# Single picks, ScalarE's copies and paired scores in the narrow attention of a two-layer decoder kernel

## The reference

```python
def _L1_attn_ref(x, g_q, Wq, bq, g_kv, Wkv, bkv, g_head, Wo, bo):
    HEAD = 16; HD = 16
    q = (_rms(x, g_q) @ Wq + bq).reshape(B, T, H, d).transpose(0, 2, 1, 3)
    kv = (_rms(x, g_kv) @ Wkv + bkv).reshape(B, T, 2, H, d)
    ...
    scores = jnp.einsum('bhqd,bhkd->bhqk', _rms(q, g_head), _rms(k, g_head)) * scale
    attn = jax.nn.softmax(scores, axis=-1)
    wv = jnp.einsum('bhqk,bhkd->bhqd', attn, v)
    out = wv.transpose(0, 2, 1, 3).reshape(B, T, D) @ Wo + bo
# the mixture's sum over the picks, which lands in x just ahead of it:
routed = jnp.einsum('enh,ne->nh', y, comb)
x = x + (routed + sg * shared)
x = x + _L1_attn_ref(_layernorm(x, axis=-1), ...)
x = x + _L1_xattn_ref(_layernorm(x, axis=-1), ctx_2048, ...)
```

## Time and profile before

| | us |
|---|---|
| median of 3 runs | 1902.86 |
| lowest and highest | 1897.18, 1907.22 |
| the profiled execution | 1888.95 |
| its span, first to last instruction | 1887.1 |
| PE busy in the span | 1651.7 (88%) |
| DVE busy | 1247.0 (66%) |
| ACT busy | 897.2 (48%) |
| POOL busy | 561.0 (30%) |

### The profile page before, as it was taken

The page is one execution under the profiler, slowest core; times in us unless marked ns, Lnnn a source line. Parts: engine busy times, 40 slices in busy tenths (PEclk is TensorE's granted clock), DMA queues, the critical chain, the costliest instruction groups (busy, mean ns, idle before and its releaser), DMA issues. The chain is left out here.

```text
span 1887.1 us, 25728 instructions
## 1 busy us (share of the span) xinstructions
PE 1651.7 (88%) x8566; PEld 1317.9 (70%) x8566; DVE 1247.0 (66%) x2655; ACT 897.2 (48%) x2548; POOL 561.0 (30%) x447
## 2 busy tenths in 40 slices
PE   6999978978998786999999877789788999999866
PEld 5878867866877665767777655667567887788644
DVE  4654775787678757544444566766557778877878
ACT  4534533433443343323322245456446666666756
POOL 2133332643253054411002554646202122211000
PEclk9999998988999988999999967879689999999989
DMA  7143432622343143233434210100021111000001
GB/s 263 63 136 126 142 104 81 215 95 95 118 143 116 71 126 100 76 99 120 129 107 134 90 45 23 34 12 23 1 106 35 39 41 41 12 1 1 1 1 45
DMA packets 87511, 151.50 MB, mean 80 GB/s; under 512 B 9940, under 2 KB 45396, under 8 KB 87380
## 3 DMA queue, kind: packets, MB, share of 16 engines
q1 hardware_dynamic: 81236, 133.07, 21.6%
q0 software_dynamic: 6144, 16.79, 2.8%
HBM read 90.84 MB, written 58.98 MB: 79 GB/s over the span
## 5 line engine op out<-in xcount | busy, mean ns | idle before, releaser
L2330 ACT ACTIVATE self_attention<-self_attention,small 128x128 f32<-128x128 f32 x256 | 100.0, 392 | 122.4 <-DVE small L1647 122.4
L2489 ACT ACTIVATE narrow_late<-bank,small 128x128 f32<-128x128 f32 x256 | 90.7, 366 | 136.2 <-DVE small L1884 136.2
L783 PE MATMUL bank<-self_attention 128*128 128x256 f32 x512 | 133.7, 408 | 12.3 <-DVE residual L1666 12.3
L2567 ACT ACTIVATE cross_attention_heads<-cross_attention_heads,small 128x128 f32<-128x128 f32 x256 | 99.6, 390 | 89.2 <-DVE small L2021 89.2
L1115 PE MATMUL bank<-cross_attention,cross_attention_heads 128*128 128x256 f32 x512 | 124.7, 387 | 15.3 <-DVE residual L2035 10.1
L783 PEld LDWEIGHTS bank<-self_attention 128*128 128x128 f32 x512 | 103.4, 206 | 32.2 <-DVE residual L1666 15.4
L2671 POOL CAST qkv_weights_split<-self_attention 128x1024 fp32r<-128x1024 f32 x45 | 50.1, 1113 | 254.5 <-DMA self_attention<-in_wqkv 197.5
L587 PE MATMUL bank<-x_channel_major,qkv_weights_split 128*128 128x512 f32 x256 | 117.9, 461 | 8.6 <-ACT self_attention L2320 4.0
L1115 PEld LDWEIGHTS bank<-cross_attention,cross_attention_heads 128*128 128x128 f32 x512 | 95.5, 191 | 38.7 <-DVE residual L2035 19.0
L2673 POOL TENSOR_TENSOR qkv_weights_split<-self_attention,qkv_weights_split 128x1024 fp32r<-128x1024 f32 x45 | 107.2, 2382 | 3.6
L881 PE MATMUL bank<-experts,tiles 128*128 x316 | 107.6, 463 | 0.2 <-DVE tiles L1773 0.2
(11 more groups left out here) (384 smaller groups left out, 4805.6 us busy)
## 6 DMA issues: line engine op xcount, KB each, us to landing
picked_inputs<-self_attention SPq DMA_DIRECT2D x64, 512.0 KB, 6.6
self_attention<-in_wqkv SPq DMA_DIRECT2D x48, 512.0 KB, 6.3
experts_far<-picked_inputs SPq DMA_DIRECT2D x79, 128.0 KB, 2.1
picked_outputs<-tiles SPq DMA_DIRECT2D x79, 128.0 KB, 1.7
self_attention<-in_wo SPq DMA_DIRECT2D x16, 512.0 KB, 4.1
experts<-in_moe SPq DMA_DIRECT2D x4, 1408.0 KB, 13.7
self_attention<-in_bv SPq DMA_DIRECT2D x16, 256.0 KB, 5.2
context_values<-context_out SPq DMA_DIRECT2D x16, 256.0 KB, 2.2
```

What stands on the lines that cost most here:

```text
L783: m = T.matmul(bank[7][:, 0:D], ZT_a[n % 2][:, h, :], wo_a[p % 2][:, h, :], start=h == 0, stop=h == HG - 1)
L2330: m = S.activation(P_a[u][:, h, :], P_a[u][:, h, :], ACT.Exp, bias=negmax_a[u][:, h:h + 1], accum_out=sums_a[u][:, h:h + 1])
L2489: m = S.activation(n_P[v][:, h, :], s4_in[:, h, :], ACT.Exp, bias=n_negmax[v][:, h:h + 1], accum_out=n_sums[bb % 2][:, q4 * 4 + h:q4 * 4 + ...
L2567: m = S.activation(P_x[u][:, h, :], P_x[u][:, h, :], ACT.Exp, bias=negmax_x[u][:, h:h + 1], accum_out=sums_x[u][:, h:h + 1])
```

## The change

The change rewrites this stretch, and one detail of the WKV chunks.

- **Picks.** The whole-batch combine in some steps becomes one pick in each of the first 32 steps (COMBINE), each with one indirect DMA a step on POOL (GATHER). Batches 0 to 7 are combined ahead of the loop instead of 0 to 3. There are four row buffers instead of three.
- **Copies.** The copy of the transposed tiles moves from DVE to ACT, ahead of the exponentials in ACT's order.
- **Scores.** The keys are spread over four heads instead of eight, so that a step's scores use 64 of the 128 rows: heads 0 to 3 of a half batch on rows 0 to 63, the next four on rows 64 to 127. PE issues the scores of an even step and the odd step after it next to each other, behind the transposes and values of the even step.
- **Bias.** The output bias is no longer added by DVE; it is cut in two fp32r parts, and PE adds it with two matmuls a batch ahead of the output projection.
- **Keys' squares.** ACT squares and sums each head of the context keys in one instruction, all of it in the first part. DVE's sums go, and there is one root and one inverse for all 16 batches.
- **Spread.** POOL's spread is half as wide and stands two steps later. The sums of a projection come a step after it on DVE, moments and norms are cut in halves over two steps. Group 0's four projections follow the last context keys instead of standing between them.
- **WKV.** PE lets 17 side steps go by before the transpose of the result, instead of 15, and none behind it instead of 2.

```diff
-NXS, NYS, NYG = 4, 3, 3
+NXS, NYS, NYG = 4, 3, 4
...
+FIRST_STEPS = [(g, 16 * (g - 1)) for g in range(1, NG)]
+MOMENTS = {n + half: (g, half) for g, n in FIRST_STEPS for half in range(2)}
+NORMALISE = {n + 2 + half: (g, half) for g, n in FIRST_STEPS for half in range(2)}
+CHANNELS = {n + 4: g for g, n in FIRST_STEPS}
+PROJECT = {n + 6 + b: GB * g + b for g, n in FIRST_STEPS for b in range(GB)}
+ROOT = {n + 11: g for g, n in FIRST_STEPS}
+HEADS = {1: 2, 2: 3, **{n + 13 + b: GB * g + b for g, n in FIRST_STEPS for b in range(GB)}}
+GATHER = {n: (9 + n // TOPK, n % TOPK) for n in range((B - 9) * TOPK)}
+COMBINE = {n: (8 + n // TOPK, n % TOPK) for n in range((B - 8) * TOPK)}
...
-                yield from pause(15)
+                yield from pause(17)
                 pe.wait_ge(wkv_y, c + 1)
                 pe.wait_ge(side_read, SIDE["y", c])
                 for b in range(GB):
                     m = T.transpose(bank[5][:, b * P:(b + 1) * P], w_y[:, b, :], ident[:, :])
                 m.then_inc(side_filled, 1)
-                yield from pause(2)
...
             def narrow_scores(n):
                 bb, q4 = divmod(n, 4)
                 pe.wait_ge(n_exp, n - 1)
                 pe.wait_ge(n_spread, bb + 1)
-                T.matmul(bank[2 + n % 2][:, :], n_qT[bb % 8][:, q4 // 2, :],
-                         kbd[bb % 2][:, q4 // 2, (q4 % 2) * 4:(q4 % 2) * 4 + 4, :].rearrange("p h t -> p (h t)"),
+                i, half = divmod(q4, 2)
+                rows = slice(half * P // 2, (half + 1) * P // 2)
+                T.matmul(bank[2 + n % 2][:, :], n_qT[bb % 8][rows, i, :], kbd[bb % 2][rows, i].rearrange("p h t -> p (h t)"),
                          start=True, stop=True).then_inc(n_scores, 1)
...
+                for part in range(2):
+                    T.matmul(bank[7][:, 256:512], ident_r, (n_bo_hi, n_bo_lo)[part], start=part == 0, stop=False)
                 for i in range(2):
-                    m = T.matmul(bank[7][:, 256:512], n_zT[bb % 2][:, i, :], n_wo[:, i, :], start=i == 0, stop=i == 1)
+                    m = T.matmul(bank[7][:, 256:512], n_zT[bb % 2][:, i, :], n_wo[:, i, :], start=False, stop=i == 1)
...
             for n in range(B * 4 + 5):
-                g, u = divmod(n, 16)
-                if n < B * 4:
-                    narrow_scores(n)
...
                 if 2 <= n < B * 4 + 2:
                     narrow_transposes(n - 2)
                 if 3 <= n < B * 4 + 3:
                     narrow_values(n - 3)
+                if n % 2 == 0 and n < B * 4:
+                    narrow_scores(n)
+                    narrow_scores(n + 1)
...
+            def narrow_transposes(n):
+                act.wait_ge(n_turned, n + 1)
+                act.wait_ge(n_values, n - 1)
+                S.copy(n_PT[n % 2], four(bank[4 + n % 2][:, :])).then_inc(n_PTs, 1)
...
+                for h in range(NKV):
+                    c = bb * NKV + h
+                    m = S.activation(bank[7][:, h * P:(h + 1) * P], x_key[bb][:, h * P:(h + 1) * P], ACT.Square,
+                                     accum_out=kss[:, c:c + 1])
```

416 lines of the change are left out of this document (211 added, 205 removed).

## The result

The changed kernel took 1876.88 us (median of 4 runs, 1874.31 to 1879.34) where the kernel before, timed beside it, took 1902.22 (1897.18 to 1907.22): a ratio of 0.9867, 95% interval 0.9837 to 0.9896, 25 us less. A later comparison with both kernels again gave 0.9859 (0.9839 to 0.9880), 28 us less. The forecast was 44 us: the sign and the range were right, the size was not.

A forecast was written before the change was run, and what follows sets the result against it. DVE, in strict order, was taken to pace the narrow attention's loop, with PE's idle time lowering the clock. Gains of 33 (loop), 0 (ahead of it) and 11 (WKV) made 1902.86 - 44 = 1859 us, range 1827 to 1885.

The forecast's parts named there:

- PE's work: Narrow attention's loop: 201 us of PE work without the half clock's cost, plus 4 for the bias matmuls.
- the pairs: Loop, two 64-row scores issued next to each other: 0 us taken, with -27 and +15 kept as bounds.
- rival of full overlap: Loop: paired scores run wholly beside each other, 27 us less work and 20 less clock, 1812 us; chance 0.10.
- The idle time: PE in the loop: 46 us against 57, from 13 + 10 + 11 + 12, before another 4 us for shorter gaps.
- no longer paces: DVE in the loop: busy sum falls from 202 to 127 us, so it stops setting the pace of the steps.
- The picks: Loop start: batch 8's gathers land late and DVE's second maximum waits behind its first pick, 10 us idle.
- The cross norms: Loop: three norms, unchanged in order, each leave PE idle for 4 us, 12 in all.
- The clock: Loop: ten gaps, 80 us at 1.2 GHz, cost 34 us instead of 56.
- The rival of a slower kernel through the clock: Loop: PE stays at 1.2 GHz longer; at a 0.70 share the kernel takes 1933 us; chance 0.07.
- ACT as the pace: Loop rival: ACT's own work sets the pace, loop 294 us, kernel 1872 us; chance 0.17.
- The part ahead of the loop: Key and value projections up to the first scores, at 1083 as before: 0 us, with 5 either way.
- The WKV transposes: WKV chunks: work put ahead of PE's wait gains 3.7 us in each of three groups, 11 us (7 to 16).

The follow-up runs named there:

- before, 3rd: The kernel before, unchanged, profiled on the same chip as the changed kernel's repeat; 1881.17 us.
- after, 3rd: The changed kernel, unchanged, run once more on the same chip as the kernel before; 1854.24 us, ratio 0.9859.
- four picks: The changed kernel with the picks of batches 8 to 15 taken four at a time again; 1833.02 us, ratio 0.9742 to the kernel before.
- division early: The changed kernel with DVE's division moved ahead of the maximum of step 4b + 6; 1856.98 us, ratio 0.9791 to the kernel before.
- pair apart: The changed kernel with the values matmuls put between the two scores of a pair; 1881.21 us, ratio 0.9994 to the kernel before.
- second profile of before: The kernel before, unchanged, profiled again; 1903.94 us.
- three moves: The changed kernel with the division earlier, batch 7's gathers behind the first spread, and cross norms one step later; 1829.81 us, ratio 0.9710 to the kernel before.

## Why the prediction was right in sign and too large

Split as the forecast split it, with half-clock time as twice (1 - clock) times the length, at 0.42 us for each us, and idle time as length less PE's busy time:

| loop of | length | PE busy | clock | work | clock cost | idle |
|---|---|---|---|---|---|---|
| before, 3rd | 311 | 259.1 | 0.78 | 202 | 57 | 52 |
| forecast | 281 | | | 205 | 34 | 42 |
| after, 3rd | 288 | 233.5 | 0.82 | 190 | 44 | 54 |
| four picks | 267 | 224.4 | 0.85 | 191 | 34 | 43 |
| division early | 270 | 235.0 | 0.81 | 192 | 43 | 35 |
| pair apart | 327 | 300.8 | 0.72 | 224 | 77 | 26 |

The clock has two digits, so work and clock cost are good to some 3 us each. Of "pair apart" only the work is to be used. The stretch tables of the two kernels of one chip, from which the first and third line come, before and then after:

```profile
1080.00:1391.00 311.00, 259.10 (x1289) 196.67 (x1289) 201.89 (x381) 158.43 (x624) 139.98 (x113) 0.78 0.07 21
...
1071.00:1359.00 288.00, 233.46 (x1328) 187.89 (x1327) 126.26 (x274) 183.26 (x677) 108.95 (x106) 0.82 0.06 19
```

- **PE's work: mis-sized, to the good.** I took 0 for the pairs, between -27 and +15, and 4 for the bias. The work fell by 12 instead of rising by 4: the pairs gave some 16 us, 0.5 a pair, nearer to the bound of -27 than to my 0. I let only one record overlap another; in the trace both scores of a pair run wholly beside each other, at 2.4 GHz as at 1.2 (1.06 us for a pair, 1.05 for one score). The rival of full overlap thus had the mechanism right. Its 27 us are too many, since a record on 64 rows takes 0.53 us instead of 0.43 and the change of mode has its price, and its time of 1812 needed a better clock as well. The page "TensorEngine Tiling (Array Packing)" of the Trainium skill, under "Key Properties", holds in both parts: tiles run in parallel, and a change of mode costs, here 0.08 to 0.18 us on the values ahead of the scores.
- **The idle time: the step that failed.** The forecast was 42 us, measured are 54, no less than before. The sentence was that with at most one pick, projection or half a norm between two maxima DVE "no longer paces". I followed one chain, scores to maxima to exponentials to values, and left out the second way by which PE hangs on DVE, the division that frees the values' bank. PE waits 36 to 39 us for it, 20 of them in nine waits that no term covers, and the kernel before paid 13 us for the same wait. The division early takes 19 us off the idle time. The same sentence fails a second time in the picks: one pick between two maxima was not harmless, and four at a time take 11 us off. The two overlap in ways that no run separates.
- **The picks: right at the start, wrong as a whole.** The first pick waited 6.0 and 6.2 us for its gather in the two profiles, as forecast, and step 8 began 36.3 and 40.5 us after step 0 against 44.2 before, so before did worse by then, as I had said (by step 4 it was the other way, 20.8 and 23.4 against 14.2). But I costed single picks as an advantage only. Taken four at a time, with everything else of the change, the loop has just the idle time and the clock cost of my forecast. That agreement is partly chance, as 33.7 us of waits for the division are still in it.
- **The cross norms** stopped PE for 5.65, 6.58 and 6.59 us, against the 4 each assumed. These are three of the twelve waits for the division, not a cost beside them. ACT's deviations come behind a step's exponentials and a key's copy, and DVE waits for them with the division and a maximum behind it:

```profile
1336.69 1.28 ACT L2200 ACT_TABLE_LOAD   x1
1337.99 0.30 ACT L2200 ACTIVATE small<-small 128x4 f32<-128x4 f32 x1
1338.32 0.18 DVE L1254 RECIPROCAL small<-small 128x4 f32<-128x4 f32 x1 [3.76 <-ACT small L2200]
1341.45 0.80 PE L1005 MATMUL bank<-narrow_attention,narrow_late 128*128 128x16 f32 x3 [6.58 <-DVE narrow_late L1916]
```

- **The clock** cost 44 us instead of 34: 104 us at 1.2 GHz where I had counted ten gaps and 80. It follows the gaps, as four picks show (34). The count was off from the start: the loop of before has 12 spells at 1.2 GHz of 3 to 24 us, 130 us in all, not 16 of about 8, and the changed one has 13. The rival of a slower kernel through the clock did not come.
- **ACT as the pace** (the 1872 of the rivals, near the measured 1877) is not the cause, though its time fits: without its 38 us of copies the kernel is no faster. A time alone proves no mechanism.
- **The part ahead of the loop**: 0 with 5 either way, measured 2.0 on one chip. That the first scores come at 1083 as before was wrong in the first profile (1093.75), as the stops in the keys and before them differ by occasion.
- **The WKV transposes**: 11 us, measured 11.4 by the end of that stage on one chip (15 and 16 in two other pairs of profiles) and 10 in the whole kernel alone. The size is right; that the whole wait would go and nearly all of it return at the output matmuls was not foreseen.
- **Behind the loop**: 0, measured +1.3.

With the forecast's own terms, 33 + 0 + 11, against the measured 23.3 - 2.0 + 11.4 - 1.3: in the loop, idle time and clock cost came out 22 us above the forecast and PE's work 15 below it, which makes 288 instead of 281 us, and the loop before is 311 on this chip, not 314. That the time fell into the range is thus in part luck: the pairs' overlap, taken at 0, paid for most of what the waits cost. Without its 16 us the kernel would have gained some 9 us instead of 25 and lain above the range.

**What stays open.** In the first profile of after, ACT and DVE stood still for some 3 us several times between 770 and 785 us, beside GpSimd's indirect DMAs, with a releaser that the trace gives only as "remote" or not at all, and PE stood still for 7.7 us. The second profile of before has the same stop, 6.9 us of PE just ahead of 798. It was not in the two profiles of the last occasion that were compared. The 10 us of the three moves that are not told apart, and four picks together with the early division, were not run. The bias on PE, the keys' squares on ACT and the narrower spread were never taken back one by one, so their shares are worked out from durations alone.

## What to carry to other kernels

When work is spread thinly over an engine that runs in strict order, list every instruction that another engine waits for, not only the one at the head of the list of waits, and look at what now stands in front of each: here the division, not the maximum. An instruction whose data may be late costs least where its data has long landed, even if four of them then come in a row. A wait of an engine that does not pace, however long, is no budget to gain from. And read a duration from all its instances: one pair of scores showed 1.47 us where 19 of 22 took 1.13 to 1.19.

## What was unexpected of the hardware

- Two fp32 scores on the two halves of the rows, side by side, cost 1.06 us at 2.4 GHz against 1.72 to 1.90 for two on all rows, and 2.01 at 1.2 GHz against 3.4 to 3.7; alone on 64 rows, one costs 1.05, plus 0.18 on the instructions ahead.
- A pick on VectorE of 0.48 us took 2.89 where GpSimd's spread began 0.55 us behind it; maxima, which read PSUM, kept their 0.69 beside a spread.
- The same kernel took 1902, 1897 and 1883 us on different occasions, two of its profiles differ by 19 us in two stretches full of indirect DMAs, and its profiled execution lay 13 us under the median of another occasion. Two single profiles should be compared by stretch, and only if both are of one occasion.
